# Routing tokens from the raw residual sums: transposes before the norm, the norm on the logits, one router product for four token tiles

## The chip, the cores and the metric

The kernel runs on one core of one Trainium2 chip. The metric is the device time of one execution in microseconds, the median of several runs. Times below that start with 20.. to 25.. are positions in the profiled execution, counted from the start of its span.

## The reference

One sequence of 4096 tokens with 512 features goes through cross attention over 3202 context rows (16 heads of 32), a residual sum, and a mixture of 8 experts of which each token uses its best two. Cut to what matters here:

```python
x = x + xattn(layernorm(x), ctx, ctx, Wq, bq, Wk, bk, Wv, bv, Wo, bo)   # ends with out @ Wo + bo

def ffn(x):                                       # x is layernorm(x), eps 1e-5, no gain, no bias
    logits = einsum('bsd,ed->bse', x, W_router) + b_router        # 8 experts
    weights = softmax(logits)
    topk_w, topk_idx = top_k(weights, 2)                          # the other six are set to 0
    expert_out = einsum('bsd,eod->bseo', x, W_experts) + b_experts
    return einsum('bseo,bse->bso', expert_out, weights)
x = x + ffn(layernorm(x))
```

All is float32. The kernel divides exp(logit - largest) of the best two by the sum over all eight, so it needs, for each token, the eight logits, their order and their exponentials.

## The kernel before

The program has four stages, one after the other, with a barrier of all engines between them: projections() makes keys, values and queries; attention() runs 32 passes over the keys and leaves the heads' outputs in DRAM, split in a high and a low part; route_tokens() is the stage of this change; mix_experts() sorts the tokens by expert, gathers their rows and multiplies. The change touches route_tokens() alone.

route_tokens() walks over 32 tiles of 128 tokens (NTL), in 8 groups (NGR) of four tiles (G4). Each engine has its own instruction stream, written out by a Python loop over steps i, in which each part of the work stands a fixed number of steps behind the projection of its tile. An engine runs its stream in order and waits at semaphores; no scheduler moves anything. The parts, by engine:

- **TensorE** (lines 1580 to 1617): project(i) multiplies the attention output by Wo, 12 products of 512 columns into one of four PSUM banks. turn(i) transposes a normalised tile, 4 transposes into a PSUM bank. route(i) multiplies the transposed tile (as weights) by the router, 4 products of 8 columns, one for each quarter of the features, added up in PSUM. turn stands 5 steps behind project, route 6.
- **VectorE** (from 1490): residual(i) adds projection and x into a tile of rows and takes its statistics; every second step it makes the low part of a piece of the expert weights (split_low). Once a group: spread() makes the four variances; scale() waits for 1/sqrt, refines it by one Newton step and writes scale and shift beside the rows, in columns 512 and 513; choose() adds the router's bias to 4 x 8 logits, and takes the best two and the running counts of tokens for each expert; weights() makes the mixing weights.
- **ScalarE** (from 1440): split_high(i) rounds a piece of the expert weights (128 x 512); normal(i) normalises a tile of rows into shared_rows, copy_turned(i) takes the transposes out of PSUM; root(q), once a group, is ln and exp with a table load before each; exps(q) the exponentials of the logits.
- **GpSimd**: adds the bias to x and makes the low parts of every second piece.
- **SP** issues the DMAs: per step a tile of x and a piece of the expert weights (256 KB each), in every second step the attention output of two tiles (two parts of 512 KB), per group one store of rows (store_rows, 1040 KB). The pieces have two buffers: the load of piece i + 2 waits for the low part of piece i, and stands behind a load of x that waits for residual(i).

What sets the order around the change is therefore the table of distances at the top (TURN, NORM, ROUTE, FIRST_STEP, SECOND_STEP), and the order of calls in the five loops. Line numbers below are those of the kernel before, if nothing else is said.

## Time and profile before

| | us |
|---|---|
| median of 3 runs | 2556.14 (2554.32 to 2556.38) |
| profiled execution | 2553.05 |
| its span | 2551.2 |
| projections and attention | up to 2073.5 |
| routing stage | 2073.8 to 2235.6 |
| expert stage | 2236.1 to 2551.2 |

The profile of one execution lists busy time of each engine: TensorE 2443.6 us (96%), VectorE 2156.9 (85%), ScalarE 1854.0 (73%), GpSimd 422.5 (17%). These shares are means over stages of different kinds, nearly all of them attention; for the routing stage the views have to be cut to its stretch, as in the rows below. In the names of the rows, wo,att_hi are project's operands, ident,shared_rows those of turn, wr,yT those of route; we_raw and we_hi are a piece of the expert weights as loaded and its high part. A matmul of float32 data shows as two records.

### The profile page before, as it was taken

How to read it: one execution, taken by the hardware profiler on the slowest of the kernel's cores; microseconds unless marked ns; L12 is line 12 of the kernel's file. 1: busy time of each engine (PE TensorE's matmuls, PEld its weight loads, DVE VectorE, ACT ScalarE, POOL GpSimd, SP SyncE). 2: the span in 40 equal slices, each digit the busy share in tenths (PEclk: the TensorE clock that was granted, in tenths of full speed). 3: DMA queues.
4: the chain of work that ended last, by engine and by line, in shares of the span. 5: the costliest groups of instructions: out<-in, count | busy, mean ns of one | idle time of the engine just before them, and what ended most of it. 6: DMA issues, size and time to landing. Idle time of an engine off the chain costs nothing. (4 is left out here: it accounts for less than half of the span.)

```text
span 2551.2 us, 37478 instructions
## 1 busy us (share of the span) xinstructions
PE 2443.6 (96%) x13675; PEld 1316.9 (52%) x13675; DVE 2156.9 (85%) x1896; ACT 1854.0 (73%) x2173; POOL 422.5 (17%) x514
## 2 busy tenths in 40 slices
PE   8999579999999999999999999999999989879998
PEld 7878334444444444444444444444444448768786
DVE  4368379999999999999999999999999976566565
ACT  3123369998999999999999998999999956513343
POOL 2113200000000000000000000000000024325664
PEclk9999789999999999999999999999999999869999
DMA  7435781111152111115111112411121048624473
...
DMA packets 141723, 231.33 MB, mean 91 GB/s; under 512 B 24902, under 2 KB 70438, under 8 KB 140780
## 3 DMA queue, kind: packets, MB, share of 16 engines
...
## 5 line engine op out<-in xcount | busy, mean ns | idle before, releaser
L1050 ACT ACTIVATE probs<-psum 128x1024 f32<-128x1024 f32 x1600 | 1513.0, 1034 | 138.5 <-PE psum L1204 131.6
L1204 PE MATMUL psum<-q_st,k_st 97*128 97x512 f32 x3200 | 923.4, 420 | 41.4 <-DMA q_st<-shift_scratch 23.5
L1204 PEld LDWEIGHTS psum<-q_st,k_st 97*128 97x128 f32 x3200 | 549.7, 189 | 617.4 <-ACT probs L1050 413.9
L1112 DVE TENSOR_TENSOR even_sums<-even_sums,probs 128x2048 f32<-128x2048 f32 x352 | 804.9, 2287 | 18.1 <-ACT probs L1050 18.0
L1225 PE MATMUL psum<-probs,v_st 128*32 128x512 f32 x6400 | 801.0, 602 | 0.0
L1112 DVE TENSOR_TENSOR odd_sums<-odd_sums,probs 128x2048 f32<-128x2048 f32 x320 | 730.6, 2283 | 1.0
L1225 PEld LDWEIGHTS psum<-probs,v_st 128*32 128x32 f32 x6400 | 152.5, 109 | 352.4 <-issue 273.4
L1912 PE MATMUL psum<-we_hi,wo 128*128 x624 | 218.9, 412 | 5.5 <-issue 5.1
...
L1765 ACT ACTIVATE wo<-psum 128x512 fp32r<-128x512 f32 x78 | 46.4, 595 | 130.9 <-PE psum L1898 130.9
L1912 PEld LDWEIGHTS psum<-we_hi,wo 128*128 128x128 f32 x624 | 119.3, 191 | 31.7 <-issue 6.1
L1912 PE MATMUL psum<-we_lo,wo 128*128 x312 | 124.6, 399 | 0.0
L1758 ACT ACTIVATE shared_rows<-hold 128x512 f32<-128x512 f32 x78 | 63.3, 812 | 65.3 <-DMA hold<-token_rows,near 35.9
L1112 DVE TENSOR_TENSOR odd_sums<-probs 128x2048 f32<-128x2048 f32 x32 | 73.3, 2292 | 30.8 <-ACT probs L1050 30.8
L342 POOL TENSOR_TENSOR squares<-o_hi 128x512 fp32r<-128x512 f32 (+1 forms) x60 | 60.5, 1016 | 208.4 <-ACT o_hi L380 120.7
L1589 PE MATMUL psum<-wo,att_hi 128*128 128x512 f32 x256 | 84.4, 412 | 6.4 <-DMA att_lo<-ol_scratch 6.4
L1112 DVE TENSOR_TENSOR even_sums<-probs 128x2048 f32<-128x2048 f32 x32 | 73.3, 2291 | 16.9 <-ACT probs L1050 16.7
L380 ACT ACTIVATE o_hi<-psum,bk_col 128x512 fp32r<-128x512 f32 (+1 forms) x28 | 17.4, 641 | 91.8 <-PE psum L595 91.8
L1822 DVE TENSOR_TENSOR res<-psum,be_all 128x512 f32<-128x512 f32 x52 | 35.9, 691 | 54.3 <-PE psum L1912 53.5
L744 POOL DMA_DIRECT2D shared_rows<-inv_scratch x124 | 61.5, 502 | 59.1 <-DMA inv_scratch<-spread_inv 59.1
L1912 PEld LDWEIGHTS psum<-we_lo,wo 128*128 128x128 f32 x312 | 59.8, 192 | 11.0
L418 ACT ACTIVATE o_hi<-psum,bq_col 128x512 fp32r<-128x512 f32 x32 | 22.0, 688 | 56.4 <-PE psum L595 56.3
...
## 6 DMA issues: line engine op xcount, KB each, us to landing
...
```

What stands on the lines that cost most here:

```text
L342: pool.tensor_tensor(squares[:, j, 0:w], h, h, ALU.mult).then_inc(squared, 1)
L418: act.activation(o_hi[b][:, j, :], psum[:, 4 + j, :], ACT.Identity, bias=bq_col[:, j:j + 1]).then_inc(q_hi, 1)
L744: pool.dma_start(a["recip"][h * DH:(h + 1) * DH, :], a["inv_d"][h:h + 1, :].to_broadcast([DH, CH])).then_inc(a["inv_in"], 16)
L1050: nc.scalar.activation(probs[:, p_slot(it, t), 2 * half:2 * half + 2, :], psum[:, 2 * slot:2 * slot + 2, :], ACT.Exp, scale=SCALE).then_in ...
L1112: nc.vector.tensor_tensor(into[:], a, probs[:, p_slot(it, t)], ALU.add).then_inc(added, 1)
L1204: mm = nc.tensor.matmul(psum[:, 2 * slot + h % 2, :], k_st[:, h, t * P:(t + 1) * P], q_st[:, b, h, :], start=True, stop=True)
L1225: mm = nc.tensor.matmul(psum[h * DH:(h + 1) * DH, bank, :], lhs(h), rhs(h), start=start, stop=stop)
L1589: mm = pe.matmul(psum[:, i % WO_BANKS, :], A[b][:, j, r, :], W[:, j, :], start=t == 0, stop=t == len(terms) - 1)
L1758: act.activation(xs[s % 2], r[:, 0:D], ACT.Identity, bias=r[:, SHIFT_AT:SHIFT_AT + 1], scale=r[:, RSTD_AT:RSTD_AT + 1]).then_inc(xs_done, 1)
L1765: act.activation(x_hi[s % 2], psum[:, T_BANK + s % 2, :].rearrange("p (k n) -> p k n", k=KT), ACT.Copy).then_inc(xh_done, 1)
L1822: dve.tensor_tensor(res[s % RES][:, 0:D], psum[:, OUT_BANKS[s % 4], :], be_all[:, ds(e, 1), :].rearrange("p o n -> p (o n)"), ALU.add).the ...
L1912: mm = pe.matmul(psum[:, OUT_BANKS[s % 4], :], A[s % 2][:, k, :], W[:, k, ds(e, 1), :].rearrange("p o n -> p (o n)"), start=t == 0, stop=t ...
```

## The change

The residual tile is transposed as it is, without the norm, 2 steps behind its projection. Since the norm is a scale and a shift for each token, a logit is scale x (raw sum of row and router column) + shift x (sum of the router column) + bias: the raw sum is made by TensorE, and the scale and the shift are applied by VectorE to the 4 x 8 logits in choose(). The sums of the router's columns are made once, at the start, by a product with a matrix of ones.

The router product is turned round: the router's quarter (8 of 32 columns filled, the rest zero) is the weight, and the transposed rows of four tiles are the moving data, 512 columns. The four quarters of features go to four sets of 32 PSUM partitions, so the array holds four tiles of 32 columns. copy_parts() on ScalarE takes the result to SBUF, and share(), four products of 8 columns with a 0/1 matrix (fold), adds the quarters and puts the tokens back on partitions. normal() goes. root() moves one step later (two for the last group), scale() goes with it into step 4q + 4, and choose() of the group before stands directly behind it. The store of rows moves from step 4q + 4 to 4q + 5. The diff, with declarations of semaphores left out:

```diff
--- before.py
+++ after.py
@@ -1309,12 +1309,14 @@
     lane, number, own, token, rows_stored = (h[n] for n in "lane number own token rows_stored".split())
     G4 = 4
     NGR = NTL // G4
-    TURN, ROUTE = 5, 6
-    NORM = 4
-    FIRST_STEP, SECOND_STEP = 10, 11
-    STEPS = (NGR - 1) * G4 + SECOND_STEP + 1
-    WO_BANKS, T_BANK, R_BANK = 4, 4, 6
+    TURN = 2
+    ROUTE, SHARE, CHOOSE, WEIGHTS = 6, 7, 8, 9
+    STEPS = (NGR - 1) * G4 + WEIGHTS + 1
+    WO_BANKS, T_BANK, PART_BANK, R_BANK = 4, 4, 6, 7
     RING = 3
+
+    def root_step(q):
+        return (q + 1) * G4 + (q == NGR - 1)
 
     with mem:
...
-        yn = [g["shared_rows"][:, b, :] for b in range(G4)]
-        yT = [sb(f"yT{b}", [P, KT, P], F32) for b in range(2)]
+        turned_rows = g["shared_rows"]
+        parts = sb("parts", [P, G4 * P], F32)
+        wr_wide = sb("wr_wide", [P, KT, DH], F32)
+        all_one = sb("all_one", [P, P], F32)
+        wr_sums = sb("wr_sums", [P, NE], F32)
+        fold = sb("fold", [P, NE], F32)
+        of_shift = sb("of_shift", [P, G4, NE], F32)
...
@@ -1404,7 +1414,7 @@
                 sp.wait_ge(results["low_ready"], LAST + 1)
                 store_result(sp, results, HEADS // HG - 1, 1, KT - 1)
                 for i in range(NTL):
-                    if i % G4 == 0 and i:
+                    if i % G4 == 1 and i > G4:
                         store_rows(i // G4 - 1)
                     if i % 2 and i // 2 + 2 < HEADS:
                         sp.wait_ge(wo_mm, i + 1)
@@ -1450,20 +1460,19 @@
                     act.wait_ge(log_ready, q + 1)
                     act.activation(rstd[:], log_var[:], ACT.Exp, scale=-0.5).then_inc(rstd_ready, 1)
 
-                def normal(i):
+                def copy_turned(i):
                     q, u = divmod(i, G4)
-                    act.wait_ge(rows_ready, q + 1)
-                    if i >= G4:
-                        act.wait_ge(turned, i - G4 + 1)
-                    r = rows[q % 2]
-                    act.activation(yn[u], r[:, u, 0:D], ACT.Identity, bias=r[:, u, SHIFT_AT:SHIFT_AT + 1],
-                                   scale=r[:, u, RSTD_AT:RSTD_AT + 1]).then_inc(yn_done, 1)
-
-                def copy_turned(i):
                     act.wait_ge(turned, i + 1)
-                    if i >= 2:
-                        act.wait_ge(routed, i - 1)
-                    act.activation(yT[i % 2][:], psum[:, T_BANK + i % 2, :].rearrange("p (k n) -> p k n", k=KT), ACT.Copy).then_inc(yT_done, 1)
+                    if u == 0 and q:
+                        act.wait_ge(parted, q)
+                    act.activation(turned_rows[:, :, u * P:(u + 1) * P], psum[:, T_BANK + i % 2, :].rearrange("p (k n) -> p k n", k=KT),
+                                   ACT.Copy).then_inc(copied, 1)
+
+                def copy_parts(q):
+                    act.wait_ge(parted, q + 1)
+                    if q:
+                        act.wait_ge(routed, q)
+                    act.activation(parts[:], psum[:, PART_BANK, :], ACT.Copy).then_inc(parts_copied, 1)
 
                 def exps(q):
                     act.wait_ge(below_ready, q + 1)
@@ -1475,17 +1484,18 @@
                 for i in range(STEPS):
                     if i < NE * KT:
                         split_high(i)
-                    if i == NORM:
+                    if i == TURN:
                         act.wait_ge(results["low_ready"], LAST + 1)
                         act.wait_ge(results["o_stored"], (LAST + 1) * STORES)
-                    if 0 <= i - NORM < NTL:
-                        normal(i - NORM)
+                    if i >= ROUTE and (i - ROUTE) % G4 == 0:
+                        copy_parts((i - ROUTE) // G4)
                     if 0 <= i - TURN < NTL:
                         copy_turned(i - TURN)
-                    if i < NTL and i % G4 == G4 - 1:
-                        root(i // G4)
-                    if i >= FIRST_STEP and (i - FIRST_STEP) % G4 == 0:
-                        exps((i - FIRST_STEP) // G4)
+                    for q in range(NGR):
+                        if i == root_step(q):
+                            root(q)
+                    if i >= WEIGHTS and (i - WEIGHTS) % G4 == 0:
+                        exps((i - WEIGHTS) // G4)
 
             @block.vector
             def _(dve):
@@ -1526,9 +1536,15 @@
                                              op0=ALU.mult, op1=ALU.mult).then_inc(rows_ready, 1)
 
                 def choose(q):
-                    dve.wait_ge(routed, (q + 1) * G4)
-                    step(dve.tensor_tensor(logits[:], psum[:, R_BANK + q % 2, 0:G4 * NE].rearrange("p (u e) -> p u e", u=G4),
-                                           br_all[:].unsqueeze(1).to_broadcast([P, G4, NE]), ALU.add))
+                    r = rows[q % 2]
+                    dve.wait_ge(rows_ready, q + 1)
+                    step(dve.tensor_tensor(of_shift[:], r[:, :, SHIFT_AT:SHIFT_AT + 1].to_broadcast([P, G4, NE]),
+                                           wr_sums[:].unsqueeze(1).to_broadcast([P, G4, NE]), ALU.mult))
+                    step(dve.tensor_tensor(of_shift[:], of_shift[:], br_all[:].unsqueeze(1).to_broadcast([P, G4, NE]), ALU.add))
+                    dve.wait_ge(routed, q + 1)
+                    step(dve.tensor_tensor(logits[:], psum[:, R_BANK, 0:G4 * NE].rearrange("p (u e) -> p u e", u=G4),
+                                           r[:, :, RSTD_AT:RSTD_AT + 1].to_broadcast([P, G4, NE]), ALU.mult))
+                    step(dve.tensor_tensor(logits[:], logits[:], of_shift[:], ALU.add))
                     for u in range(G4):
                         ins = dve.max(top[:, u, :], logits[:, u, :])
                         n[0] += 1
@@ -1557,25 +1573,37 @@
                 dve.wait_ge(results["o_left"], LAST + 1)
                 dve.tensor_tensor(results["o_sb"], results["o_sb"], results["recip"], ALU.mult).then_inc(results["o_final"], 1)
                 dve.wait_ge(small_in, 48)
+                step(dve.memset(wr_wide[:], 0.0))
+                dve.tensor_copy(wr_wide[:, :, 0:NE], wr[:]).then_inc(router_ready, 1)
+                dve.memset(all_one[:], 1.0).then_inc(router_ready, 1)
                 step(dve.memset(before[:, 0], 0.0))
                 for b in range(2):
                     step(dve.memset(rows[b][:, :, D:ROW], 0.0))
                 dve.wait_ge(results["high_ready"], LAST + 1)
                 dve.tensor_tensor(results["o_low"], results["o_sb"], results["o_high"].bitcast(F32), ALU.subtract).then_inc(results["low_ready"], 1)
                 dve.wait_ge(counted, 4)
+                step(dve.tensor_tensor(fold[:], ident[:, 0:NE], ident[:, DH:DH + NE], ALU.add))
+                for k in range(2, KT):
+                    ins = dve.tensor_tensor(fold[:], fold[:], ident[:, k * DH:k * DH + NE], ALU.add)
+                    if k == KT - 1:
+                        ins.then_inc(router_ready, 1)
+                    else:
+                        step(ins)
+                dve.wait_ge(wr_summed, 1)
+                step(dve.tensor_copy(wr_sums[:], psum[:, R_BANK, 0:NE]))
                 for i in range(STEPS):
                     if i < NTL:
                         residual(i)
                         if i % 2 == 0:
                             split_low(dve, i, we_lo_dve)
-                    if i >= FIRST_STEP and (i - FIRST_STEP) % G4 == 0:
-                        choose((i - FIRST_STEP) // G4)
                     if i < NTL and i % G4 == G4 - 1:
                         spread(i // G4)
-                    if i >= SECOND_STEP and (i - SECOND_STEP) % G4 == 0:
-                        weights((i - SECOND_STEP) // G4)
-                    if i < NTL and i % G4 == G4 - 1:
-                        scale(i // G4)
+                    if i >= G4 and i % G4 == 0 and i <= NTL:
+                        scale(i // G4 - 1)
+                    if i >= CHOOSE and (i - CHOOSE) % G4 == 0:
+                        choose((i - CHOOSE) // G4)
+                    if i >= WEIGHTS and (i - WEIGHTS) % G4 == 0:
+                        weights((i - WEIGHTS) // G4)
 
             @block.tensor
             def _(pe):
@@ -1590,30 +1618,48 @@
                     mm.then_inc(wo_mm, 1)
 
                 def turn(i):
-                    pe.wait_ge(yn_done, i + 1)
+                    q, u = divmod(i, G4)
+                    pe.wait_ge(y_done, i + 1)
                     if i >= 2:
-                        pe.wait_ge(yT_done, i - 1)
+                        pe.wait_ge(copied, i - 1)
                     for k in range(KT):
-                        mm = pe.transpose(psum[:, T_BANK + i % 2, k * P:(k + 1) * P], yn[i % G4][:, k * P:(k + 1) * P], ident[:])
+                        mm = pe.transpose(psum[:, T_BANK + i % 2, k * P:(k + 1) * P], rows[q % 2][:, u, k * P:(k + 1) * P], ident[:])
                     mm.then_inc(turned, 1)
 
-                def route(i):
-                    q, u = divmod(i, G4)
-                    pe.wait_ge(yT_done, i + 1)
-                    if u == 0 and q >= 2:
-                        pe.wait_ge(below_ready, q - 1)
+                def route(q):
+                    pe.wait_ge(copied, (q + 1) * G4)
+                    if q == 0:
+                        pe.wait_ge(router_ready, 3)
+                    else:
+                        pe.wait_ge(parts_copied, q)
                     for k in range(KT):
-                        mm = pe.matmul(psum[:, R_BANK + q % 2, u * NE:(u + 1) * NE], yT[i % 2][:, k, :], wr[:, k, :], start=k == 0, stop=k == KT - 1)
+                        mm = pe.matmul(psum[k * DH:(k + 1) * DH, PART_BANK, :], wr_wide[:, k, :], turned_rows[:, k, :], start=True, stop=True)
+                    mm.then_inc(parted, 1)
+
+                def share(q):
+                    pe.wait_ge(parts_copied, q + 1)
+                    if q:
+                        pe.wait_ge(below_ready, q)
+                    for u in range(G4):
+                        mm = pe.matmul(psum[:, R_BANK, u * NE:(u + 1) * NE], parts[:, u * P:(u + 1) * P], fold[:], start=True, stop=True)
                     mm.then_inc(routed, 1)
 
                 pe.wait_ge(small_in, 48)
-                for i in range(NTL + ROUTE):
+                for i in range(STEPS):
                     if i < NTL:
                         project(i)
+                    if i == 0:
+                        pe.wait_ge(router_ready, 2)
+                        pe.wait_ge(results["o_final"], LAST + 1)
+                        for k in range(KT):
+                            mm = pe.matmul(psum[:, R_BANK, 0:NE], all_one[:], wr[:, k, :], start=k == 0, stop=k == KT - 1)
+                        mm.then_inc(wr_summed, 1)
                     if 0 <= i - TURN < NTL:
                         turn(i - TURN)
-                    if 0 <= i - ROUTE < NTL:
-                        route(i - ROUTE)
+                    if i >= ROUTE and (i - ROUTE) % G4 == 0 and i - ROUTE < NTL:
+                        route((i - ROUTE) // G4)
+                    if i >= SHARE and (i - SHARE) % G4 == 0 and i - SHARE < NTL:
+                        share((i - SHARE) // G4)
 
 
 def mix_experts(nc, mem, sb0, sem, psum, ident, g, h):
```

VectorE before, in the steps where a group ends and the next begins (L1551 to L1553 are weights(), L1521 to L1525 scale(), L1506 and L1508 residual() with its statistics, L1377 split_low()):

```order
L1551 TENSOR_REDUCE total<-ex 128x4
L1552 RECIPROCAL inv<-total 128x4
L1553 TENSOR_TENSOR mix<-ex,inv 128x8
L1521 TENSOR_TENSOR tmp<-rstd 128x4
L1522 TENSOR_TENSOR tmp<-tmp,var 128x4
L1523 TENSOR_SCALAR tmp<-tmp 128x4
L1524 TENSOR_TENSOR rows<-rstd,tmp 128x4
L1525 SCALAR_TENSOR_TENSOR rows<-mv,rows 128x4
L1506 TENSOR_TENSOR rows<-psum,xb 128x512
L1508 BN_STATS stats<-rows 128x6
L1377 TENSOR_TENSOR we_lo<-we_raw,we_hi 128x512
```

VectorE after, from the end of scale() (L1535) over choose() (L1541 to L1563) to the next residual (L1516):

```order
L1535 SCALAR_TENSOR_TENSOR rows<-mv,rows 128x4
L1541 TENSOR_TENSOR of_shift<-rows,wr_sums 128x32
L1543 TENSOR_TENSOR of_shift<-of_shift,br_all 128x32
L1545 TENSOR_TENSOR logits<-psum,rows 128x32
L1547 TENSOR_TENSOR logits<-logits,of_shift 128x32
L1549 MAX top<-logits 128x8 x4
L1553 TENSOR_TENSOR below<-top 128x32
L1555 MAX_INDEX top_at<-top,logits 128x8 x4
L1559 CAST at<-top_at 128x8
L1560 TENSOR_TENSOR picked<-number,at 128x64
L1563 TENSOR_TENSOR picked_before<-picked_before,picked 128x16 x4
L1516 TENSOR_TENSOR rows<-psum,xb 128x512
```

Behind scale() the next residual came at once; now 17 operations of choose() for the group before stand between them, and weights() follows behind that residual.

SP before, around the store of a group's rows (L1395; xb is a tile of x, we_raw a piece, att_hi and att_lo the attention output):

```order
L1395 DMA token_rows<-rows 128x4x520
L1383 DMA xb<-in_x 128x512
L1391 DMA we_raw<-in_WeT 128x512
L1387 DMA att_hi<-oh_scratch 128x1024
L1387 DMA att_lo<-ol_scratch 128x1024
L1383 DMA xb<-in_x 128x512
L1391 DMA we_raw<-in_WeT 128x512
L1383 DMA xb<-in_x 128x512
L1391 DMA we_raw<-in_WeT 128x512
```

SP after, the same place in its stream (the store is L1405):

```order
L1393 DMA xb<-in_x 128x512
L1401 DMA we_raw<-in_WeT 128x512
L1405 DMA token_rows<-rows 128x4x520
L1397 DMA att_hi<-oh_scratch 128x1024
L1397 DMA att_lo<-ol_scratch 128x1024
L1393 DMA xb<-in_x 128x512
L1401 DMA we_raw<-in_WeT 128x512
L1393 DMA xb<-in_x 128x512
L1401 DMA we_raw<-in_WeT 128x512
```

One load of x and one of a piece went ahead of the store; the loads of the attention output follow it directly.

## Rows read from the trace of the kernel before

**Rows 1.** Windows: start:end, length, busy time of each engine, PEclk, DMA share, GB/s
```profile
2079.50:2212.40 132.90, 127.26 (x688) 105.86 (x689) 82.55 (x277) 72.98 (x119) 59.96 (x47) 0.98 0.86 303
2212.40:2235.60 23.20, 14.52 (x82) 14.24 (x80) 11.16 (x68) 10.56 (x18) 1.29 (x1) 0.61 0.12 47
```

**Rows 2.** Waits from 2055 to 2245: waiter, releaser: us in total, times, longest
```profile
ACT we_hi L1445 <- DMA we_raw<-in_WeT: 53.8, 17, 7.4
...
PE psum L1597 <- ACT shared_rows L1459: 10.4, 7, 5.3
```

**Rows 3.** Timeline of SP: start, us, engine, line, DMA issued
```profile
2092.40 0.33 SPq L1391 DMA_DIRECT2D we_raw<-in_WeT  x1
...
2100.20 0.38 SPq L1395 DMA_DIRECT2D token_rows<-rows  x1
...
2134.25 0.38 SPq L1395 DMA_DIRECT2D token_rows<-rows  x1
...
2150.74 0.38 SPq L1395 DMA_DIRECT2D token_rows<-rows  x1
...
2219.62 0.38 SPq L1395 DMA_DIRECT2D token_rows<-rows  x1
```

**Rows 4.** Timeline of TensorE, one tile step
```profile
2139.44 0.60 PE L1597 MATMUL psum<-ident,shared_rows 128*128 128x128 f32 x4
2139.88 0.96 PE L1606 MATMUL psum<-wr,yT 128*128 128x8 f32 x8
2140.69 0.71 PE L1589 MATMUL psum<-wo,att_hi 128*128 128x512 f32 x2
...
2143.57 0.60 PE L1597 MATMUL psum<-ident,shared_rows 128*128 128x128 f32 x4
```

**Rows 5.** Timeline of ScalarE from the arrival of a piece to rstd
```profile
2144.78 0.63 ACT L1445 ACTIVATE we_hi<-we_raw 128x512 fp32r<-128x512 f32 x1 [1.57 <-DMA we_raw<-in_WeT]
2145.32 0.80 ACT L1459 ACTIVATE shared_rows<-rows 128x512 f32<-128x512 f32 x1
2146.03 0.57 ACT L1466 ACTIVATE yT<-psum 128x512 f32<-128x512 f32 x1
...
2149.43 0.21 ACT L1451 ACTIVATE rstd<-log_var 128x4 f32<-128x4 f32 x1
```

**Rows 6.** Timeline of TensorE in attention, a set of 32-column products and the next
```profile
2061.45 1.07 PE L1225 MATMUL psum<-probs,v_st 128*32 128x512 f32 x8
2062.44 1.82 PE L1204 MATMUL psum<-q_st,k_st 97*128 97x512 f32 x6
```

**Rows 7.** Timeline of VectorE, one group
```profile
2142.14 0.18 DVE L1530 TENSOR_TENSOR logits<-psum,br_all 128x32 f32<-128x32 f32 x1
...
2144.84 0.69 DVE L1506 TENSOR_TENSOR rows<-psum,xb 128x512 f32<-128x512 f32 x1
...
2146.30 0.38 DVE L1513 BATCH_NORM_AGGREGATE mv<-stats 128x2 f32<-128x6 f32 x4
...
2147.21 0.86 DVE L1553 TENSOR_TENSOR mix<-ex,inv 128x8 f32<-128x8 f32 x1
...
2150.65 0.69 DVE L1506 TENSOR_TENSOR rows<-psum,xb 128x512 f32<-128x512 f32 x1
...
2151.99 0.67 DVE L1377 TENSOR_TENSOR we_lo<-we_raw,we_hi 128x512 fp32r<-128x512 f32 x1
```

**Rows 8.** Tile we_raw in the stage: DMA from issue to landing
```profile
DMA to landing us min/median/max: 3.3/4.6/7.4
```

**Rows 9.** Windows, columns as in rows 1: the loaded part of two groups, and a burst
```profile
2135.00:2149.40 14.40, 14.40 (x89) 12.46 (x88) 9.91 (x37) 8.88 (x15) 7.58 (x6) 1.00 1.01 364
2186.50:2201.80 15.30, 15.30 (x91) 13.20 (x92) 9.77 (x37) 8.60 (x14) 7.59 (x6) 1.00 0.97 343
2140.00:2143.00 3.00, 3.00 (x19) 2.60 (x18) 2.43 (x11) 1.83 (x4) 1.27 (x1) 1.00 1.03 419
```

**Rows 10.** Timeline of VectorE, the last operation of the routing stage
```profile
2235.43 0.17 DVE L1553 TENSOR_TENSOR mix<-ex,inv 128x8 f32<-128x8 f32 x1
```

7 lines of the change are left out of this document (5 added, 2 removed).

## The prediction

> **What bounds the kernel now.** I read the time by stage first. Nearly all of the span is attention, which the edit doesn't touch; the edit lives in the routing stage. [rows 1] cut that stage in two: 2079.5 to 2212.4, where TensorE is busy 127.3 of 132.9 us and the DMA engines 86%, and a tail to 2235.6, where TensorE is busy 14.5 of 23.2 us at a mean granted clock of 0.61 (partly at 1.2 GHz, not 2.4) and DMA is almost quiet. So at first sight TensorE bounds the long part and a chain bounds the tail.
>
> Then the waits. [rows 2]: ScalarE stood 53.8 us for pieces of the expert weights, TensorE only 10.4 us for normalised rows, 7 times, once a group of four token tiles. The stage has eight groups, and the stores of their rows show their pace: [rows 3] have the first at 2100.20 and the last (the eighth) at 2219.62, so 17.06 us a group; the undisturbed one from 2134.25 takes 16.49.
>
> TensorE's own work in a tile step [rows 4]: transposes 0.44 us (2139.44 to 2139.88), router product 0.81 (to 2140.69), output projection 2.88 (to 2143.57). Four steps are 16.5 us. The pace of the groups is between this and something longer, so I looked for a loop, going back from a store of rows, in the timelines of SP, ScalarE and VectorE. It needs scale() on VectorE; that needs root() on ScalarE, queued behind split_high of a piece; the piece was issued by SP behind the previous store. From the issue of the store at 2134.25 to the arrival of the piece at 2144.78 [rows 3, 5] are 10.5 us, in which the queue moves 3.1 MB (the store 1040 KB, four loads of 256 KB, a pair of 512 KB each); from there to the next store 5.96. Their sum is the 16.49. So this loop through DMA, ScalarE, VectorE and SP is as long as TensorE's work: taking work from TensorE alone gives nothing unless the loop gets shorter too.
>
> **The change part by part.**
>
> TensorE, per group. Removed: four router products, 4 x 0.81 = 3.24. Added: route(), four products of 32 columns of weights over 512 tokens, side by side, and share(), four products of the old shape, 0.82. What route() costs is shown by attention [rows 6]: eight records of that shape from 2061.45, the next product at 2062.44, so 0.99. New sum: 4 x (0.44 + 2.88) + 0.99 + 0.82 = 15.1 us a group, 1.4 under before. The bounds of route(): 0.82, what four small products cost, and 4 x 0.99 = 4.0, if the four would not overlap; I take 0.99, since that row is the same shape and type.
>
> On this the Trainium skill ("TensorEngine Tiling (Array Packing)", Key Properties) has two rules: column tiles run independently of each other, and a change of tiling mode drains the engine. The second speaks against the edit, which adds two changes of mode per group. The 0.99 of [rows 6] already holds the way back to a full-width product, so the trace leaves little room for the drain; by the first rule without the second the group would be at most 0.2 shorter, and without the first it would be 18.1.
>
> ScalarE. normal() (0.71 from row to row, 2145.32 to 2146.03 [rows 5]) goes, four a group; one copy_parts of 0.6 comes. The two table loads a group stay. But root() moves one step later: it now sits behind split_high(4q+4) and copy_turned, no longer behind split_high(4q+3).
>
> VectorE. choose() gets three more small operations, 0.21 each: 2.70 (2142.14 to 2144.84 [rows 7]) becomes 3.33. It used to stand in a step of its own; now it comes directly behind scale(), and both stand before residual(4q+1), as the order in the section on the change shows.
>
> SP. The store of rows stood ahead of the loads of step 4q; now it stands behind two of them, directly ahead of load_o in step 4q+1.
>
> **The new loop**, from A, the arrival of piece 4q (start of its split_high):
> - to the end of scale(): A to the rstd instruction is 4.65 (2144.78 to 2149.43), less 0.71 for normal(), then 1.22 to the next residual (2149.43 to 2150.65) [rows 5, 7]: 5.16
> - choose(): 3.33
> - residual(4q+1) and statistics, 2144.84 to 2146.30 [rows 7]: 1.46
> - weights(): 0.63 if its three parts are as short as other small operations, 0.21 each, 1.3 with the 0.86 of the last part in the row; I take 0.9
> - residual(4q+2), statistics, split_low, and SP's issue: 1.34 + 0.7 = 2.04
> - arrival of piece 4q+4: 3.3 us at the least, 4.6 in the median, 7.4 at the most [rows 8]
> The first five are 12.9. The landing I take from the queue: a group moves 5.24 MB (364 GB/s x 14.4 us), and the engines need 14.4 us for it in a good group and about 15.3 in a late one [rows 9]; of the 2.1 us a group in which they stand idle now (16.49 less 14.4) I leave 1.3, since the store still comes when the queue is nearly empty. That gives 15.7 to 16.6, so the piece lands 3.3 to 3.7 after its issue: a period of 16.2 to 16.6. I take 16.3, and for the range 15.8 to 17.1. TensorE (15.1) then waits about 1.2 us a group, in turn(4q+1) for residual(4q+1).
>
> The start. The sums of the router weights cost TensorE four products (0.8 to 1.6 at the lower clock) and hold residual(0) by about 1.3 us. Piece 4, issued at 2092.40 before [rows 3], goes out at about 2093.5 and lands about 5 later: A1 = 2099 (2097 to 2101). The first interval has no choose() and no weights(); there TensorE's 15.1 decides: A2 = 2114.1. Five more intervals: A7 = 2114.1 + 5 x 16.3 = 2195.6.
>
> The tail, counted from A7: scale 5.16, choose 8.49, statistics of tile 29 9.95, weights 10.85, tile 30 with its split 12.86, residual(31) 13.55. Then turn(31) and copy to 15.1 (0.9 and 0.6), root 2.95 to 18.1, scale 19.1, choose(6) 22.4, weights 23.1, choose(7) 26.4, weights 27.0. The two group products and copy_parts lie beside scale and choose(6). End of the stage: 2195.6 + 27.0 = 2222.6. Before it ended at 2235.6 [rows 10]. What has gone is the file of four transposes, copies and router products at a lowered clock behind the last scale(). The last store, issued about A7 + 19, needs some 5 us and is inside.
>
> Gain 2235.6 - 2222.6 = 13.0 us: about 4 from the pace, 9 from the tail less the start. Everything behind the stage is the same work, from the same idle start; I cost it at nothing. The profiled execution was 2553.05 (span 2551.2 and 1.85 around it), so 2540; the median of the runs was 2556.14, 3.1 higher, so I predict 2543 for the runs.
>
> **Rivals.**
> 1. The pace doesn't move, only the tail: period 17.06, A7 = 2199.4, end 2226.4, gain 9.2: 2547. For it: the median landing of 4.6 would make the loop 17.5. Against: the store now goes out 12.9 - 5.2 = 7.7 us ahead of the piece that closes the loop, so most of what was queued ahead of that piece has moved by then.
> 2. TensorE or DMA is the floor: period 15.1, A7 = 2189.6, end 2216.6, gain 19.0: 2537. It needs VectorE's 12.9 to be 1 us too long. For it: three us at 419 GB/s [rows 9]. The Trainium skill ("DMA: Bandwidth & Descriptors", Bandwidth) gives 341 GB/s for a transfer of 1 MB and 425 for 16 MB; by the latter 5.24 MB would take an estimated 12.3 us and this rival would hold, by the former 15.4 and it would not. The trace has 364 over a whole group, nearer to the former.
> 3. Slower: scale and choose in front of residual(4q+1) make the loop long, and the piece lands in a full queue. With the largest landing of [rows 8], 7.4, the period is 20.3: A7 = 2215.6, end 2242.6, 7 us slower: 2563. It turns slower where the period passes 18.9, since (2235.6 - 27.0 - 2114.1) / 5 = 18.9; that is a landing of 6.0. Against: such landings occurred in the burst behind a store only.
> 4. The side by side product isn't side by side: route() 4.0, TensorE 18.1 a group, all six intervals at that: A7 = 2207.6, end 2234.6, gain 1.0: 2555. Against: [rows 6].
>
> **How the numbers follow.** Forecast (period 15.8 to 16.7, gain 11 to 15.5) 0.47; rival 1 (16.7 to 18) 0.26; rival 2 0.14; rival 3 0.07; rival 4 0.02; tail or start off by more than 6 us 0.04. A change of 0.2%, 5.1 us, is what a measurement of this kernel can tell from none. Forecast, rival 2 and nearly all of rival 1 are faster by more: 0.87; same: 0.07 (rival 4, the ends of 1 and 3); slower: 0.06. The range goes from rival 2, 2536.5, to a gain of 5, 2551.
>
> **What would show it.** The stores of rows about 16.3 us apart, from about 2104; TensorE waiting about a microsecond once a group for a residual, and no more for normalised rows; a group product of 32 columns at 0.99; ScalarE waiting less for pieces; the stage ended 27 us behind the last group's first piece. The prediction is wrong if the stores stay 17 us apart (then rival 1), if they are 15 apart with TensorE full (2), or if the DMA engines are idle several us a group while VectorE is in choose() (3).

## The result, and the profile after

The changed kernel takes 2563.45 us in the median of 7 runs (2561.93 to 2568.24), the kernel before 2556.28 in 7 runs beside it (2554.32 to 2560.77). The ratio is 1.0031, with an interval of 1.0021 to 1.0041: slower, by more than 0.2%. The forecast was 2543, with a range from 2536.5 to 2551. The profiled execution took 2561.93 (span 2560.1), against 2553.05 (2551.2).

The stage, in windows of the changed kernel (start:end, length, busy time of PE, PEld, DVE, ACT and POOL, PEclk, DMA share, GB/s):

```profile
2079.50:2212.40 132.90, 120.69 (x572) 92.84 (x573) 89.72 (x270) 53.20 (x92) 55.54 (x44) 0.91 0.84 284
2217.40:2241.70 24.30, 11.17 (x56) 6.94 (x48) 18.37 (x95) 8.06 (x15) 3.77 (x4) 0.67 0.28 99
...
2100.00:2200.00 100.00, 89.12 (x427) 67.58 (x424) 68.62 (x218) 42.09 (x73) 39.82 (x32) 0.90 0.80 274
```

Against [rows 1] TensorE does less in the same time, at a granted clock of 0.91 and not 0.98, ScalarE has lost a quarter of its work, and DMA moves 284 GB/s and not 303. No engine is fuller than before except VectorE. The stores of rows, from SP's timeline, against [rows 3]:

```profile
2101.70 0.38 SPq L1405 DMA_DIRECT2D token_rows<-rows  x1
...
2217.36 0.38 SPq L1405 DMA_DIRECT2D token_rows<-rows  x1
...
2241.62 3.66 SPq L1744 DMA_DIRECT2D be_all<-in_be  x8
```

Six intervals from 2101.70 to 2217.36 are 19.28 us each in the mean (18.0 to 20.4); before they were 17.18 by the same count. The last row is the first DMA of the next stage: 2241.62, where it was 2236.10 in the kernel before. So 5.5 us of the 8.9 in the two spans arose here. The other 3.4 lie in the expert stage, which no edit touches; from that DMA to the end of the span it took 315.1 us in the kernel before and from 313.2 to 322.9 in the experiments, whatever their order, so I put nothing down to it.

The waits of the changed kernel from 2055 to 2245 (waiter, releaser: us in total, times, longest), against [rows 2]:

```profile
ACT we_hi L1455 <- DMA we_raw<-in_WeT: 59.4, 21, 7.3
ACT ex L1479 <- DVE below L1553: 29.4, 8, 4.6
...
DVE rows L1516 <- POOL xb L1438: 19.4, 8, 5.0
DVE tmp L1531 <- ACT rstd L1461: 15.7, 8, 3.5
...
PE psum L1617 <- DMA att_lo<-ol_scratch: 12.4, 9, 6.1
PE psum L1626 <- DVE rows L1516: 10.1, 7, 2.2
```

TensorE's wait for normalised rows has gone and two others have come: for the residual of tile 4q+1, as forecast, and for the attention pair, which wasn't. (Of the 12.4 us for the pair, 6.1 are the start of the stage, and the kernel before waits 6.0 there too; behind it the changed kernel waits 6.3 more, the kernel before 0.4.) To see why a group takes 19.3 us, here is one turn of the loop that the prediction had summed, from one piece's arrival to the arrival of the piece four later (timeline of the changed kernel, rows of several engines):

```profile
2139.77 0.38 SPq L1405 DMA_DIRECT2D token_rows<-rows  x1
2140.74 1.01 SPq L1397 DMA_DIRECT2D att_lo<-ol_scratch  x1
2147.48 1.22 PE L1617 MATMUL psum<-wo,att_hi 128*128 128x512 f32 x2 [0.47 <-DMA att_lo<-ol_scratch]
2151.69 0.60 PE L1626 MATMUL psum<-ident,rows 128*128 128x128 f32 x4
2153.08 0.63 ACT L1455 ACTIVATE we_hi<-we_raw 128x512 fp32r<-128x512 f32 x1 [3.04 <-DMA we_raw<-in_WeT]
2153.61 0.58 ACT L1468 ACTIVATE shared_rows<-psum 128x512 f32<-128x512 f32 x1
2157.02 0.20 ACT L1461 ACTIVATE rstd<-log_var 128x4 f32<-128x4 f32 x1
2157.97 1.29 POOL L1387 TENSOR_TENSOR we_lo<-we_raw,we_hi 128x512 fp32r<-128x512 f32 x1 [4.56 <-ACT we_hi L1455]
2158.06 1.22 DVE L1535 SCALAR_TENSOR_TENSOR rows<-mv,rows 128x4 f32<-128x4 f32 x1
2159.21 0.18 DVE L1541 TENSOR_TENSOR of_shift<-rows,wr_sums 128x32 f32<-128x32 f32 x1
2159.22 2.55 POOL L1438 TENSOR_TENSOR xb<-xb,bo_all 128x512 f32<-128x512 f32 x2
2159.31 0.38 SPq L1405 DMA_DIRECT2D token_rows<-rows  x1
2159.42 1.15 DVE L1543 TENSOR_TENSOR of_shift<-of_shift,br_all 128x32 f32<-128x32 f32 x1
2160.83 0.99 DVE L1547 TENSOR_TENSOR logits<-logits,of_shift 128x32 f32<-128x32 f32 x1
2164.35 0.69 DVE L1516 TENSOR_TENSOR rows<-psum,xb 128x512 f32<-128x512 f32 x1
2168.34 0.33 SPq L1401 DMA_DIRECT2D we_raw<-in_WeT  x1
2172.43 0.63 ACT L1455 ACTIVATE we_hi<-we_raw 128x512 fp32r<-128x512 f32 x1 [2.83 <-DMA we_raw<-in_WeT]
```

From 2153.08 to 2172.43 are 19.35 us. I call this the first ring: piece(4q+4), split_high, root, scale, choose, residual(4q+5) and (4q+6), split_low, the next piece. There is another way around, which the prediction never wrote down, and the first rows show it: the store at 2139.77 is directly ahead of an attention pair (att_lo issued 2140.74), TensorE projects from it at 2147.48, only then turns tile 4q+2 (2151.69), ScalarE copies that at 2153.61, and root stands behind the copy; root releases scale, and scale the next store, at 2159.31. This second ring needs 19.54 us here, of which some 1.3 are slack, since the copy could have begun at the end of the turn, 2152.3, and stood behind the piece of 2153.08.

### The profile page after: what moved, and what is told of

It reads as the page before. It is cut to its first block and busy times, and to the rows that moved or that the text cites. A ratio compares the mean times of both kernels' runs of the same rounds, so it can differ in the third digit from the quotient of the medians.

```text
span 2560.1 us, 37213 instructions
## 1 busy us (share of the span) xinstructions
PE 2437.6 (95%) x13555; PEld 1298.3 (51%) x13555; DVE 2173.9 (85%) x1927; ACT 1835.5 (72%) x2149; POOL 422.3 (16%) x514
## 5 line engine op out<-in xcount | busy, mean ns | idle before, releaser
L734 POOL DMA_DIRECT2D sum_scratch<-shared_rows x31 | 18.3, 590 | 1211.9 <-ACT shared_rows L1005 1211.9
L1617 PE MATMUL psum<-wo,att_hi 128*128 128x512 f32 x256 | 89.3, 432 | 12.4 <-DMA att_lo<-ol_scratch 12.4
L1617 PEld LDWEIGHTS psum<-wo,att_hi 128*128 128x128 f32 x256 | 49.8, 205 | 30.2 <-issue 12.8
## 6 DMA issues: line engine op xcount, KB each, us to landing
token_rows<-in_x SPq DMA_DIRECT2D x1, 8192.0 KB, 30.1
```

What stands on the lines that cost most here:

```text
L1617: mm = pe.matmul(psum[:, i % WO_BANKS, :], A[b][:, j, r, :], W[:, j, :], start=t == 0, stop=t == len(terms) - 1)
```

## The experiments

"Period" is the mean of the first six intervals between stores, and the stage's end is the first DMA behind it. Both come from one profiled execution of each kernel, the ratios from the medians of several, so the two needn't agree closely: e13 ends its stage 2.1 us later than the changed kernel and has the lower ratio. Ratios are to the kernel before on the same chip. The kernels are the changed one with the edit that is named, unless said otherwise; where choose or weights come later, copy_parts has also got an upper bound, so that the longer loop doesn't call it once too often.

| run | edit | ratio | interval | period | stage's end |
|---|---|---|---|---|---|
| before | | 1 | | 17.18 | 2236.10 |
| changed | | 1.0031 | 1.0021 to 1.0041 | 19.28 | 2241.62 |
| e1 | choose later | 1.0042 | 1.0029 to 1.0056 | 20.23 | 2245.07 |
| e2 | little work for GpSimd | 0.9961 | 0.9947 to 0.9975 | 17.31 | 2228.61 |
| e3 | root, scale, store back | 0.9981 | 0.9972 to 0.9990 | 17.35 | 2231.01 |
| e4 | three piece buffers | 1.0057 | 1.0043 to 1.0071 | 20.62 | 2250.25 |
| e5 | e3, choose later | 0.9978 | 0.9968 to 0.9989 | 17.23 | 2229.82 |
| e6 | choose by way of PSUM | 1.0036 | 1.0023 to 1.0049 | 20.28 | 2248.13 |
| e7 | store behind piece | 1.0036 | 1.0023 to 1.0049 | 20.14 | 2250.40 |
| e8 | kernel before, as e2 | 0.9986 | 0.9978 to 0.9995 | 17.18 | 2234.62 |
| e9 | root alone back | 0.9966 | 0.9953 to 0.9979 | 16.72 | 2226.94 |
| e10 | e9, choose later | 1.0027 | 1.0017 to 1.0037 | 19.64 | 2242.49 |
| e11 | e5, store at 4q+5 | 1.0010 | 1.0002 to 1.0019 | 18.45 | 2238.28 |
| e12 | choose later, pair ahead of store | 0.9956 | 0.9943 to 0.9969 | 17.00 | 2229.12 |
| e13 | pair ahead of store | 1.0009 | 1.0000 to 1.0018 | 19.12 | 2243.71 |
| e14 | root back, pair ahead | 0.9975 | 0.9964 to 0.9987 | 17.98 | 2235.46 |
| e15 | e14, choose 10, weights 12 | 0.9947 | 0.9935 to 0.9960 | 16.95 | 2228.60 |
| e16 | e14, low parts all on DVE | 0.9976 | 0.9966 to 0.9986 | 17.22 | 2231.59 |
| e17 | root back, choose 10, weights 12 | 0.9948 | 0.9934 to 0.9961 | 16.62 | 2223.92 |
| e18 | e15 as e2 | 0.9947 | 0.9933 to 0.9960 | 16.80 | 2225.01 |

**e1, choose moved alone.**

```diff
-    ROUTE, SHARE, CHOOSE, WEIGHTS = 6, 7, 8, 9
+    ROUTE, SHARE, CHOOSE, WEIGHTS = 6, 7, 10, 11
```

> The changed kernel with choose() two steps later (behind split_low of step 4q+2 instead of directly behind scale() in step 4q), weights() with it. Theory L (the loop store - choose - residual - piece - root - scale sets the pace, 19.3 us a group, of which choose() is 5.1): period falls to the next floor, 15.5 to 16.5 us, some 19 us in six intervals, time about 2545. Rival D (the order of the store in the DMA queue costs the time: it goes out with the loads of the attention output directly behind it): no change, period 19, 2563. Rival T (TensorE loses time in the new product or in changes of shape): no change either.

1.0042: choose's 5.1 us left the first ring, and the period, for which 15.5 to 16.5 had been expected, rose to 20.23. What sets it now stands in the timeline of that run, once around the second ring, with the window of the projection in it:

```profile
2160.94 0.38 SPq L1405 DMA_DIRECT2D token_rows<-rows  x1
2161.90 1.03 SPq L1397 DMA_DIRECT2D att_lo<-ol_scratch  x1
2168.80 1.22 PE L1617 MATMUL psum<-wo,att_hi 128*128 128x512 f32 x2 [2.06 <-DMA att_lo<-ol_scratch]
2174.08 0.77 PE L1626 MATMUL psum<-ident,rows 128*128 128x128 f32 x4
2174.89 0.60 ACT L1468 ACTIVATE shared_rows<-psum 128x512 f32<-128x512 f32 x1 [2.71 <-PE psum L1626]
2178.32 0.20 ACT L1461 ACTIVATE rstd<-log_var 128x4 f32<-128x4 f32 x1
2179.12 1.29 POOL L1387 TENSOR_TENSOR we_lo<-we_raw,we_hi 128x512 fp32r<-128x512 f32 x1 [4.43 <-ACT we_hi L1455]
2179.15 1.29 DVE L1534 TENSOR_TENSOR rows<-rstd,tmp 128x4 f32<-128x4 f32 x1
2180.48 1.21 DVE L1535 SCALAR_TENSOR_TENSOR rows<-mv,rows 128x4 f32<-128x4 f32 x1
2181.71 0.38 SPq L1405 DMA_DIRECT2D token_rows<-rows  x1
```

```profile
2168.80:2174.08 5.28, 5.28 (x12) 4.02 (x13) 1.30 (x9) 1.86 (x4) 3.14 (x3) 0.50 1.04 404
```

Store to store are 20.77 us, without slack: ScalarE waited for the turn and SP for scale. The projection took 5.28 us at a granted clock of 0.50, 1.2 GHz; TensorE had been busy for 1.0 of the 3.8 us ahead of it. In the turn of the changed kernel the same projection took 4.21 (2147.48 to 2151.69) at a mean clock of 0.65, and L1534 0.17 and not 1.29. These two, 1.07 and 1.12 us, are most of the 2.55 by which this turn is longer than the 18.2 above. I read these rows in this way only behind the next runs.

**e2 and e8, little work for GpSimd** (e2 the changed kernel, e8 the kernel before, with the same edit; both leave out the attention bias and half of the low parts):

```diff
-                    pool.tensor_tensor(xb[i % RING][:], xb[i % RING][:], bo_all[:], ALU.add).then_inc(xb_done, 1)
+                    pool.tensor_tensor(xb[i % RING][:, 0:8], xb[i % RING][:, 0:8], bo_all[:, 0:8], ALU.add).then_inc(xb_done, 1)
...
-                        split_low(pool, i, we_lo_pool)
+                        k, e = piece(i)
+                        pool.wait_ge(we_hi_ready, i + 1)
+                        pool.memset(we_lo[:, k, e, :].bitcast(F32), 0.0).then_inc(we_lo_pool, 1)
```

> The changed kernel with GpSimd's two operations made harmless: the bias is added to 8 columns only and the low part of the odd pieces is set to zero instead of computed (so the attention bias and half of the low parts are left out). Theory P (small VectorE operations with two SBUF inputs wait for the end of a GpSimd operation; in scale() and choose() that costs about 2.9 us a group): the long ones of 1.0 to 1.2 us in L1535, L1543 and L1547 fall to 0.2, the period to about 16.4, time about 2546. Rival (they are long for another reason, DMA writes or semaphores): they stay at 1.0 to 1.2 us, period 18 or more.

> The kernel before with GpSimd's bias on 8 of 512 columns and its low parts of odd pieces set to zero (leaves out the attention bias and half of the low parts), as the second run did with the changed kernel, which became 0.7% faster. Contention theory says the gain there came from the new operations that stand in the loop beside GpSimd; in the kernel before, where those lie off the loop, the same edit gives little: 2550 to 2555 (DVE's wait for xb, 1.2 us in all, and mix). Rival: GpSimd's work costs every order of this stage about the same, and before gains 15 to 18 us too: 2537 to 2540.

The changed kernel gained 0.7% by it (1.0031 to 0.9961), the kernel before 0.14%. So GpSimd's work costs something in the new order that it hardly cost in the old one. What that is can be read in the turn above: L1535 ran 1.22 us, until GpSimd's split of 2157.97 ended, and L1543 and L1547, 1.15 and 0.99, ended with the two additions of 2159.22; the same three take 0.17 to 0.19 where GpSimd is quiet. The Trainium skill ("SBUF — State Buffer", Who interferes with whom) says that an instruction of VectorE with two inputs in SBUF contends with one of GpSimd that reads SBUF, and that the loser blocks for the whole of it. The trace agrees, with 0.8 to 1.05 us each. I call such a stretched operation held.

e2's trace also says how long the second ring is when nothing is held:

```profile
2137.92 0.38 SPq L1405 DMA_DIRECT2D token_rows<-rows  x1
2145.69 1.22 PE L1619 MATMUL psum<-wo,att_hi 128*128 128x512 f32 x2 [1.62 <-DMA att_lo<-ol_scratch]
2150.14 0.60 PE L1628 MATMUL psum<-ident,rows 128*128 128x128 f32 x4
2150.77 0.60 ACT L1470 ACTIVATE shared_rows<-psum 128x512 f32<-128x512 f32 x1 [0.57 <-PE psum L1628]
2154.20 0.21 ACT L1463 ACTIVATE rstd<-log_var 128x4 f32<-128x4 f32 x1
2155.43 0.38 SPq L1405 DMA_DIRECT2D token_rows<-rows  x1
```

From store to store are 17.51 us, without slack, and the period of the run is 17.31, not the 16.3 of the forecast and not the 16.4 expected of this run.

**e3 and e5, root, scale and store where they were** (scale behind weights in VectorE's step 4q+3; e5 has e1's hunk besides).

```diff
-        return (q + 1) * G4 + (q == NGR - 1)
+        return q * G4 + G4 - 1
-                    if i % G4 == 1 and i > G4:
+                    if i % G4 == 0 and i:
                         store_rows(i // G4 - 1)
-                    if i >= G4 and i % G4 == 0 and i <= NTL:
-                        scale(i // G4 - 1)
...
+                    if i < NTL and i % G4 == G4 - 1:
+                        scale(i // G4)
```

> The changed kernel with root() and scale() back in step 4q+3 and the store in step 4q+4, as before the change; transposes of raw rows, the side by side product and share() stay; choose() stays in step 4q+8, alone there. Theory L: store to store is then the old loop less normal() (15.8), but choose() now stands ahead of residual(4q+5), behind which the closing piece is issued: 16.5 to 17.3 us a group; with the shorter tail 2545 to 2550. Rival T: period stays near 19, time over 2560.

> The changed kernel with both moved back: root and scale as in the kernel before (at steps 4q+3, store at 4q+4), and choose and weights at steps 4q+10 and 4q+11, where the kernel before had them. Placement theory (the loss comes from scale and choose standing ahead of residual(4q+1), which the placing of root alone brought back to 17.35 us per group and 2548): choose behind residual(4q+2) takes its 4 to 6 us off the way to the x load and to split_low(4q+2), so 16.5 us per group and 2541 to 2545. Queue rival (the order of the transfers sets the pace, choose's place does nothing, as in the run with choose moved alone): 17.3 us per group, 2548 again.

0.9981: the new product with the old place of the norm is faster than the kernel before. e5 is the same (0.9978); choose's place is worth nothing there, where 16.5 us a group had been expected of it. In neither trace is an operation of scale held by more than 0.2 us.

**e4, three buffers for the pieces**, each piece loaded three steps ahead and not two (two semaphores are merged and a constant shares its memory, to make room):

```diff
+    PR = 3
...
-                    if i + 2 < NE * KT:
+                    if i + PR < NE * KT:
                         lo_of_piece(sp, i)
-                        load_piece(i + 2)
+                        load_piece(i + PR)
```

> The changed kernel with three buffers for the pieces of the expert weights instead of two (piece i+3 is issued where i+2 was). Theory L: root() no longer waits for a landing; the loop goes on through the tile of x (issued behind residual(4q+1), then GpSimd, then residual(4q+4)): period 16.5 to 17.5, ScalarE's wait for pieces under 20 us of 59, time about 2548. Rival D (the queue itself is too slow): pieces still land late, period 19.

1.0057, period 20.62, where 16.5 to 17.5 had been expected: earlier pieces made it slower. The second ring again: store at 2145.39, att_lo issued 2146.36, first projection 2153.11, turn 2158.40, copy 2159.07, store 2165.88; the window from 2153.11 to 2158.40 has a clock of 0.50. The pair came 6.75 us behind its issue, as in the changed kernel (6.74); what is longer is the projection, 5.29 us for 4.21, and L1534, held for 1.29. This run sank the idea that the piece's landing was the limit and made me look for another way around.

**e6, no two-input operations in choose's logits** (the sums, the bias and the shift term are kept in PSUM bank 7):

```diff
+        wr_sums = psum[:, R_BANK, 64:64 + NE]
+        br_bank = psum[:, R_BANK, 80:80 + NE]
...
```

> The changed kernel with every operation of choose's logits reading at least one operand from PSUM (the sums of the router's columns, its bias and the shift term lie in bank 7), so that no DVE operation with two SBUF inputs is left there until below. Contention theory (two-input DVE operations of choose wait for GpSimd's split and bias additions): L1543's 1.15 and L1547's 0.99 us fall to 0.19, the loop turn of 19.35 us loses up to 1.8 us, minus what the hold then catches of the next operations: about 18 us per group and 2553 to 2557. Queue rival: 19.3 per group and 2563 unchanged. If the hold only moves to the next two-input operation: 2561 to 2564.

1.0036. From 2100 to 2200 of its trace the two operations take 196 and 187 ns instead of 964 and 669, so the hold is gone where it was aimed at, and the period is 20.28 all the same; the 18 us expected by contention missed. But the hold has moved, into scale, where it lies in both rings. In the four groups from 2110 to 2190 both L1534 and L1535 (here L1536 and L1537) are held in every one, 2.1 us a group, while the changed kernel has 1.6: L1535 in all four, L1534 in two. e1 and e4 have 2.1 too. So e1, e4 and e6, each of which shortens the first ring alone, end at 20.2 to 20.6 in the same way: the second ring holds, TensorE waits for the pair (10.7 us in the 78 from 2118 to 2196 in e6, 9.0 in e1, 3.2 in the changed kernel), and scale is held twice.

**e7, the store behind pair, x and piece of step 4q+5:**

```diff
                         lo_of_piece(sp, i)
                         load_piece(i + 2)
+                    if i % G4 == 1 and i > G4:
+                        store_rows(i // G4 - 1)
```

> The changed kernel with the store of 1.04 MB behind the attention pair, the x load and piece(4q+3) of SP's step 4q+1 instead of ahead of them. Queue rival (attention and x land late because the store lies ahead of them, and TensorE waits): 1 to 2 us per group less, 2550 to 2556. Contention and placement theory (scale and choose on DVE, held by GpSimd, set the turn): the period stays near 19.3 and the time at 2560 to 2565, or somewhat worse, since the store then delays piece(4q+4), which closes the loop.

1.0036, nothing won, as the placement theory had it. This one doesn't isolate the second ring, since it delays the store's own landing, for which VectorE now waited (3.2 us in 78), and it leaves the first ring whole.

**e9, root alone.** If there are two rings, their common part is root.

```diff
     def root_step(q):
-        return (q + 1) * G4 + (q == NGR - 1)
+        return q * G4 + G4 - 1
```

> The changed kernel with one edit: ScalarE's root(q) one step earlier, at step 4q+3 (behind copy_turned(4q+1)), so ahead of split_high(4q+4) and copy_turned(4q+2); scale, store, choose and weights stay where the change put them. Theory of the two rings: in the changed kernel a group turns in two rings of nearly one length, piece(4q+4) -> split_high -> root -> scale -> choose -> residual(4q+5) and (4q+6) -> split_low -> load (19.35 us in the turn read), and store -> attention pair -> project(4q+8), (4q+9) -> turn -> copy_turned -> root -> scale -> store (19 to 20.5); root lies in both, and taking it out of them frees some 3.4 us of the first (both table loads) and cuts the second at copy_turned: 17 to 17.6 us per group and 2547 to 2551 (ratio to before 0.997 to 0.999). If instead scale's and choose's place on DVE is what costs, root's place alone gives little: 2560 to 2566 (ratio 1.002 to 1.004).

0.9966, period 16.72, a little better than expected: one line takes 0.65% off the changed kernel. Scale, store and choose stand where the change put them. The line does two things, though: root leaves both rings, and nothing in scale is held any more, since split_high(4q+5) and with it GpSimd's split no longer come directly behind root. e9 alone can't tell them apart; the next two runs can.

**e12 and e13, the rings opened elsewhere.** Root stays late. e13 has only the second hunk, e12 both:

```diff
-    ROUTE, SHARE, CHOOSE, WEIGHTS = 6, 7, 8, 9
+    ROUTE, SHARE, CHOOSE, WEIGHTS = 6, 7, 10, 11
...
-                    if i % G4 == 1 and i > G4:
-                        store_rows(i // G4 - 1)
                     if i % 2 and i // 2 + 2 < HEADS:
                         ...
                         load_o(i // 2 + 2)
+                    if i % G4 == 1 and i > G4:
+                        store_rows(i // G4 - 1)
```

> The changed kernel with its root left where it is, but both rings opened elsewhere: choose and weights at 4q+10 and 4q+11 (out of the first ring) and, in SP's step 4q+5, the attention pair issued ahead of the store (the second ring no longer begins at scale). Each edit alone is worth nothing by the ring theory, since the other ring then holds (choose alone: ratio 1.0042 measured). Both: the first ring is 19.35 - 5.1, so 15 to 17.5 us per group with the queue, 2545 to 2553 (ratio 0.996 to 1.000). If the second ring isn't what held the run with choose alone, this one stays with it: 1.003 to 1.005.

> The changed kernel with one edit: in SP's step 4q+5 the attention pair is issued ahead of the store. Theory of the two rings: the second ring no longer begins at scale, but the first (19.35 us from piece to piece, with choose in it) is untouched: 18.5 to 19.5 us per group, ratio 1.001 to 1.004. Rival: one ring only, the one from the store; then this edit alone gives what the run with both edits gave, 0.9956.

Choose alone 1.0042, pair alone 1.0009 (period 19.12, as the rings have it; the time is 0.2% under the changed kernel's, just below what was expected), both 0.9956. Two edits of which each alone leaves the period at 19 to 20 us and both together give 17.0: that is what two rings of nearly one length do, and one ring of which each edit takes a part can't. The holds alone don't explain it: in the five groups from 2110 to 2200 the operations of scale are held 1.3 us a group in e12, as much as in the changed kernel in the same stretch, and the period is 17.0 and not 19.3. In e12 TensorE's wait for att_lo fell to 0.4 us in the 78 from 2118 to 2196.

**e10, e11 and e17, a third ring.** e10 is e9 with choose and weights at 10 and 11, e11 is e5 with the store at 4q+5, e17 is e10 with weights at 12:

> As the run before it (root at step 4q+3 of ScalarE, scale and store where the change put them), and choose and weights at steps 4q+10 and 4q+11. Ring theory: with root out of the rings, choose at 4q+8 would be the next piece of the first ring (5.1 us); here it is gone too, so 16 to 17 us per group and 2540 to 2547 (ratio 0.994 to 0.997). Queue rival (the 5.1 MB per group at the share of 0.88 that the best runs reach bounds them all near 17.3): no better than the run before it or the one with root, scale and store moved back (ratio 0.998).

> Root and scale where the kernel before had them, choose at 4q+10, but the store at SP's step 4q+5, as the change has it: SP no longer stops at step 4q+4 for rows_ready, which kept it from issuing anything for 4.8 us of a turn (from piece at 2163.59 to the store at 2168.36) while the queue ran empty. If that stop is what holds the pace at 17.3 us: 16.3 to 16.8 and 2540 to 2545 (ratio 0.994 to 0.996). If x(4q+7), which waits for residual(4q+4) behind scale on DVE, stops SP just as long: 17.3 and ratio 0.998.

e10 missed: 1.0027, where 0.994 to 0.997 had been expected. ScalarE's and VectorE's timelines of e10 say why:

```profile
2148.06 0.63 ACT L1455 ACTIVATE we_hi<-we_raw 128x512 fp32r<-128x512 f32 x1 [7.96 <-DMA we_raw<-in_WeT]
2148.60 0.58 ACT L1468 ACTIVATE shared_rows<-psum 128x512 f32<-128x512 f32 x1
2149.19 1.28 ACT L1459 ACT_TABLE_LOAD   x1
...
2152.00 0.20 ACT L1461 ACTIVATE rstd<-log_var 128x4 f32<-128x4 f32 x1
2152.11 0.21 ACT L1479 ACTIVATE ex<-below 128x32 f32<-128x32 f32 x1
...
2152.36 0.19 DVE L1567 TENSOR_REDUCE total<-ex 128x4 f32<-128x32 f32 x1 [5.13 <-ACT ex L1479]
...
2153.00 0.69 DVE L1516 TENSOR_TENSOR rows<-psum,xb 128x512 f32<-128x512 f32 x1
```

At step 4q+11 the exponentials stand on ScalarE behind a piece and behind root(q+2), and the weights that need them stand on VectorE ahead of residual(4q+12): piece, root, exponentials, weights, residual, split_low, piece. e17 moves them one step:

```diff
-    ROUTE, SHARE, CHOOSE, WEIGHTS = 6, 7, 10, 11
+    ROUTE, SHARE, CHOOSE, WEIGHTS = 6, 7, 10, 12
```

> The run with root at 4q+3 and choose at 4q+10 (1.0027), with one edit: exponentials and weights at 4q+12 instead of 4q+11. If DVE's wait for the exponentials (19.8 us of 78 there, behind piece(4q+11) and root on ScalarE) was a third ring, it is gone: 16.5 to 17.2 us per group, ratio 0.995 to 0.999. If the store ahead of the attention pair is what it stays with, 1.001 to 1.003.

0.9948 against 1.0027. e11 has the same wait (18.3 us of 78 for the exponentials), which is enough to say nothing of its store.

**e14 to e16 and e18, what is left.** e14 is e9's hunk with e13's, e15 has `CHOOSE, WEIGHTS = 10, 12` besides, e18 is e15 with e2's hunks, and e16 is e14 with GpSimd's split taken out and

```diff
-                        if i % 2 == 0:
-                            split_low(dve, i, we_lo_dve)
+                        split_low(dve, i, we_lo_dve)
```

> The changed kernel with root at step 4q+3 of ScalarE and the attention pair ahead of the store. Root alone gave 0.9966 with TensorE waiting 5.6 us for att_lo in 78. Those waits go if the pair is no longer behind the store's wait: 16.2 to 16.7 us per group, ratio 0.993 to 0.996. If the first ring (scale and choose ahead of residual(4q+5)) is what holds it: 16.7 and 0.9966 again.

> As e14, and choose at 4q+10 with the exponentials and weights at 4q+12, so that the exponentials stand on ScalarE behind split_high(4q+12) and not behind root(q+2). With root and choose both moved and weights at 4q+11, DVE waited 19.8 us in 78 for the exponentials (1.0027); if that is what cost there, this one runs at 16 to 16.5 us per group, ratio 0.992 to 0.995; if choose behind residual(4q+6) costs by itself (it delays residual(4q+7) and root), 0.997 to 1.000.

> As e14, with the low parts of the odd pieces on DVE too, in place of GpSimd: 2 x 0.68 us more for DVE in a group, 2 x 1.28 less for GpSimd, and no split of GpSimd's beside scale and choose. Contention theory (the two-input DVE operations are held for a whole GpSimd operation, 1.2 us each, 4 of them in a group): up to 3 us less against 1.4 more, 0.5 to 1.5 us per group better than e14, and odd pieces no longer wait for GpSimd's bias additions. Rival (DVE is what the ring runs through, each 0.68 counts): 1 us per group slower than e14.

> The fastest correct order (root at 4q+3, attention pair ahead of the store, choose at 4q+10, weights at 4q+12; 0.9947) with GpSimd's bias on 8 of 512 columns and its low parts set to zero (leaves out the attention bias and half of the low parts). There DVE waited 20 us of 78 for xb, the x load and GpSimd's addition behind it. If GpSimd's own time is that wait, 15.5 to 16 us per group and 0.991 to 0.993; if the x loads' landing is it, 0.994 to 0.995.

With root early the pair ahead of the store wins nothing (e14 0.9975 beside e9's 0.9966, where 0.993 to 0.996 had been expected; e15 0.9947 beside e17's 0.9948). All low parts on VectorE give the same time as e14 (0.9976); the profiled periods, 17.22 against 17.98, differ by the 0.5 to 1.5 us that were expected, but e14's profiled execution took 3.7 us more than its median, so I put nothing down to that. And e18: with the rings open, taking GpSimd's work away wins nothing (0.9947 again). The best order that leaves nothing out is e17 (or e15), 2541.87 us (2539.24 to 2543.29) beside 2554.58 of the kernel before. Its stores, and a hundred us of it as a window:

```profile
2101.30 0.38 SPq L1405 DMA_DIRECT2D token_rows<-rows  x1
...
2201.05 0.38 SPq L1405 DMA_DIRECT2D token_rows<-rows  x1
...
2223.92 3.65 SPq L1744 DMA_DIRECT2D be_all<-in_be  x8
```

```profile
2100.00:2200.00 100.00, 95.47 (x481) 73.52 (x480) 70.33 (x248) 48.55 (x84) 45.39 (x36) 0.95 0.91 318
```

Open: its 16.6 us are still 1.5 above TensorE's sum of 15.1. TensorE is busy for 95.5 of the 100 us at a mean clock of 0.95, DMA is at 0.91, and VectorE waits for x with its bias, 11.5 us in 78; in e18, where the bias is next to nothing, it still waits 10.8 (20.0 in e15), and that part is the arrival of x. I didn't run a kernel with less to transfer, so whether the transfers set this isn't shown.

## Why the prediction was wrong

- **TensorE's sum: right.** The group product was costed at 0.99 us; in the changed kernel it begins at 2140.38 and the next product at 2141.37: 0.99. The rival that it would not run side by side is out.
- **"The new loop": the first ring was right in its members and too short in three terms.** By the turn above: A to rstd 3.94, as summed. From rstd to the end of scale 2.19 against 1.22: L1535 was held. choose 5.14 against 3.33: 1.76 of the 1.81 are L1543 and L1547. residual(4q+1) 1.34 against 1.46, weights 0.61 against 0.9, the rest 2.04 as summed. The landing 4.09 against 3.4. In all 19.35 against 16.3. The prediction costed the new small operations at 0.21 each from a row (L1530) that reads PSUM and ran beside a quiet GpSimd; the 0.86 of mix in [rows 7] was the hint that the same kind of operation can take four times as long, and was read as a detail of weights. In the new order root releases GpSimd's split (behind split_high(4q+5)) and VectorE's scale at the same moment, so they met in each of the four groups from 2110 to 2190.
- **The step that failed: that this loop was the only one beside TensorE's own work.** The working put the store "directly ahead of load_o" and noted root "behind split_high(4q+4) and copy_turned", and drew nothing from either. copy_turned(4q+2) waits for TensorE, TensorE for the pair, the pair for the store, the store for the scale of the group before. In the turn shown that ring has 18.2 us without its slack, of which 1.05 are the hold on L1535, and e2, where nothing is held, has it at 17.5 and a period of 17.31: the period could not have been 16.3 even with every term of the first ring as summed. e9, e12 and e13 show that there are two rings; e1, e4 and e6 show that where the second one holds it is 20 to 21 us, for TensorE waits in it and then runs the projection at half clock, 5.3 us for 2.9, and scale is held twice.
- **Rival 3** had the right sign, the right sum (2563) and the right place, scale and choose ahead of residual(4q+1), but another price: a landing of 7.4 us. The landing was 4.1. It was held at 0.07 since only its landing was asked about, and neither the holds nor a second ring. That its 2563 is the measured time is luck: its period was 20.3 for 19.28, its tail 3.1 us short, and 3.4 us of the difference between the two spans lie in the expert stage.
- **The tail.** Forecast 27.0 us from A7; A7 was 2211.05 and VectorE's last operation ended at 2241.1, so 30.1. With the pace the other way: 2211.05 and not 2195.6. The stage's end came 18.5 us late against 2222.6, of which 15.4 had gathered by A7 and 3.1 are the tail. Of these, 2.9 are L1535, L1543 and L1547 once more, held in the group that begins at A7 (1.29, 1.16 and 0.99 us).
- **The gain that was foretold is there.** e17 has the same products, copies and sums as the changed kernel, and its stage ends at 2223.92, 12.2 us ahead of the kernel before, where 13.0 were foretold; its period of 16.6 is near the 16.3. What took it away, and 0.3% more, is the place of root on ScalarE, with the rings and the holds that come of it; choose and the exponentials then had to be placed apart as well to get all of it.

How the 3.0 us between 16.3 and 19.28 are shared out is settled only so far. Without GpSimd's work (e2) 2.0 of them go, and the ratio falls by 0.7%; the 1.0 that stays is the second ring. e6 takes away choose's two holds, gets another in scale, and gains nothing; e18 takes all away with the rings open and gains nothing. That fits if the hold on scale, which lies in both rings, is the part that counts; but no run takes away that one alone, and e2 also brings x earlier to VectorE, so this share isn't shown.
